# A fused attention and expert kernel: the SP queue and the scatters reordered, new weights for the order of steps, and the last two groups of heads taken by halves of the queries

## The reference, cut to what matters

```python
x = L0_attn_x
x = _layernorm(x + _L0_attn_ref(x, ...))      # 8 heads of 16, causal softmax, a rank-one term per head in the scores
x = _layernorm(x + _L0_ffn_ref(x, ...))

def _L0_ffn_ref(x, ...):
    x = x + mla_attention(rmsnorm(x, norm1_w), ...)   # latent of 64, 16 heads of 8, rotary, causal softmax
    x = x + moe(rmsnorm(x, norm2_w), ...)
    return x

def moe(x, gate_w, gate_b, W1, b1, W2, b2):
    logits = x @ gate_w.T + gate_b
    top = jnp.argmax(logits, axis=-1)
    onehot = jax.nn.one_hot(top, N_EXPERTS, dtype=x.dtype)     # 4 experts, hidden width 512
    h = jax.nn.relu(jnp.einsum('btd,ehd->bteh', x, W1) + b1)
    y = jnp.einsum('bteh,edh->bted', h, W2) + b2
    return jnp.einsum('btd,bte->btd', y, onehot)
```

## Time and profile before

| | |
|---|---|
| three runs, us | 559.97, 563.38, 565.47 (median 563.38) |
| the profiled execution | 565.1 us, its span in the trace 563.4 us |
| busy in the span | PE 480.2 us (85%), DVE 371.9 (66%), ACT 323.6 (57%), POOL 179.8 (32%) |
| granted PE clock, mean | 0.95 of full speed |

### The profile page before, as it was taken

One profiled execution on the slowest core, in us unless ns is written; L12 is line 12 of the kernel. 1 busy time (PEld: TensorE's weight loads), 2 busy tenths in 40 slices (PEclk: granted clock), 3 DMA queues, 4 the chain that ended last, 5 costly groups with the idle time before them and its releaser, 6 DMA issues.

```text
span 563.4 us, 10237 instructions
## 1 busy us (share of the span) xinstructions
PE 480.2 (85%) x3749; PEld 223.4 (40%) x3764; DVE 371.9 (66%) x690; ACT 323.6 (57%) x488; POOL 179.8 (32%) x249
## 2 busy tenths in 40 slices
PE   5576799998899989888797998848888988999993
PEld 3242233444442333333232333312554443367762
DVE  4286977788877889688888788866356721233343
ACT  3422156576676668867685776715456677843331
POOL 9830131237554237634030222452202304601000
PEclk9977889999999999999999799976899999999998
DMA  3894030306112002012010102031000000100010
GB/s 96 214 210 132 2 96 23 94 1 243 45 56 65 25 5 83 28 52 65 17 43 9 52 3 58 6 98 45 6 12 15 8 12 20 30 1 0 20 38 20
DMA packets 31571, 28.83 MB, mean 51 GB/s; under 512 B 8017, under 2 KB 27857, under 8 KB 31250
## 3 DMA queue, kind: packets, MB, share of 16 engines
q1 hardware_dynamic: 30626, 26.34, 16.3%
q0 software_dynamic: 896, 1.84, 1.4%
HBM read 19.27 MB, written 9.31 MB: 51 GB/s over the span
## 4 chain that ended last, share of the span: by engine, by line
PE 58%; ACT 10%; DVE 10%; SPq 8%; issue 5%; DMA 4%; POOL 3%; ACTq 1%; another core or an unknown queue 0%; DVEq 0%; POOLq 0%
PE ps L1407 15%; PE ps L1390 10%; ACT pr L1607 7%; PE ps L1370 7%; DVE mparts L1887 6%; PE ps L1486 5%; PE ps L1542 5%; SPq L1018 4%; PE ps L1472 3%; SPq L1088 3%; DMA qs<-nparts 2%; PE ps L1466 2%; PE ps L1586 2%; PE ps L1574 2%; PE ps L1418 2%
## 5 line engine op out<-in xcount | busy, mean ns | idle before, releaser
L1887 DVE TENSOR_REDUCE mparts<-ps 128x2 f32<-128x1024 f32 (+3 forms) x240 | 260.4, 1114 | 83.0 <-PE ps L1370 78.5
L1607 ACT ACTIVATE pr<-ps 128x1024 f32<-128x1024 f32 (+1 forms) x240 | 221.2, 939 | 142.9 <-PE ps L1390 140.6
L1407 PE MATMUL ps<-pr,vs 128*32 128x512 f32 (+3 forms) x1152 | 124.4, 506 | 9.1 <-ACT pr L1607 5.7
L1390 PE MATMUL ps<-qs,ks 64*128 64x512 bf16 (+7 forms) x561 | 102.1, 339 | 21.1 <-DMA qs<-nparts 11.3
L1370 PE MATMUL ps<-ks,qs 61*128 61x512 bf16 (+7 forms) x576 | 108.7, 348 | 4.0 <-DVE mparts L1887 1.9
L1208 POOL TENSOR_SCALAR_AFFINE_SELECT pr<-pr 128x512 f32<-128x512 f32 x96 | 60.7, 635 | 156.5 <-ACT pr L1607 156.3
L1390 PEld LDWEIGHTS ps<-qs,ks 64*128 64x128 bf16 (+1 forms) x576 | 31.5, 96 | 106.7 <-issue 41.6
L1370 PEld LDWEIGHTS ps<-ks,qs 61*128 61x128 bf16 (+1 forms) x576 | 35.5, 101 | 33.3 <-ACT pr L1607 11.0
L1407 PEld LDWEIGHTS ps<-pr,vs 128*32 128x32 f32 x1152 | 23.6, 108 | 48.5 <-issue 30.1
L1711 ACT ACTIVATE work<-ps,b 128x512 f32<-128x512 f32 x32 | 21.8, 685 | 29.7 <-PE ps L1542 28.2
L1363 PE MATMUL ps<-cmask,identb 64*128 64x128 bf16 (+1 forms) x96 | 23.4, 244 | 11.8 <-DVE mparts L1887 4.8
(11 more groups left out here) (174 smaller groups left out, 563.5 us busy)
## 6 DMA issues: line engine op xcount, KB each, us to landing
qs<-scr0q SPq DMA_DIRECT2D x48, 64.0 KB, 2.4
qs<-scr1q SPq DMA_DIRECT2D x84, 32.0 KB
ks<-scr1k SPq DMA_DIRECT2D x84, 32.0 KB
ks<-scr0k SPq DMA_DIRECT2D x36, 64.0 KB, 2.3
scr0q<-parts SPq DMA_DIRECT2D x4, 384.0 KB, 3.1
scr0k<-parts SPq DMA_DIRECT2D x4, 384.0 KB, 3.6
scr1q<-parts SPq DMA_DIRECT2D x4, 384.0 KB, 2.5
scr1k<-parts SPq DMA_DIRECT2D x4, 384.0 KB, 2.7
```

The costliest lines, as they stand in the source:

```text
L1390: last = pe.matmul(to[:, k, h, :], keys(F, 3, 2 * k + h0 + h, j * P, P), queries(F, 3, 2 * k + h0 + h, qb * 512 + lo, n), start=True, stop ...
L1407: last = pe.matmul(ps[VW * h:VW * (h + 1), PVB, lo:lo + n], vs[:, F % VSLOTS, j, VW * h:VW * (h + 1)], pr[:, st % PSLOTS, h, 0:n], start=( ...
L1607: act.activation(heads, scores_at(F, v), ACT.Exp, scale=GROUPS[F][0].scale).then_inc(exped, 1)
L1887: dve.tensor_reduce(heads, maxes_at(F, u), AX_X, ALU.max).then_inc(taken, 1)
```

## The change

The table of numbers that makes the list is new, and with it the places of most steps; beside that the diff changes these things.

- `query_halves()` and `SEQUENCE`: groups 10 and 11 are a pair (`PAIRED`). Their order is 10 q = 0, 11 q = 0, 10 q = 1, 11 q = 1. The maxima of group 11 are combined, turned and written in two halves, each with 12 DMAs (`rows`, four quarters of the rows). `serial()` gives the buffers of the exponentials in the new sequence; `ot` and `rc` alternate by it.
- `rows` of groups 4 to 10: three DMAs of two rows each in the place of six of one row.
- `MOST` allows three pairs of banks for scores and maxima and four single ones for the rest.
- The first half of group 0's keys is loaded from the SP queue, no longer from POOL.
- From the third on, a scatter waits until the one two before it has landed (two semaphores).
- `tile_out` on PE and `tile_relu` on ACT read the expert's number ahead of their waits.
- `hidden` waits for its own features, and is placed behind the last `tile_store`.

```diff
+PAIRED = [(10, 11)]
+ROWS_HALVED = [0] + [second for _, second in PAIRED]
...
-MOST = {"scores": 2, "row maxima": 2, "turns": 2, "side": 3}
+MOST = {"scores": 3, "row maxima": 3, "turns": 2, "side": 4}
...
+def query_halves():
+
+    out, F = [], 0
+    while F < NF:
+        groups = (F, F + 1) if (F, F + 1) in PAIRED else (F,)
+        out += [(G, q) for q in range(2) for G in groups]
+        F += len(groups)
+    return out
+
+
+SEQUENCE = query_halves()
+
+
+def serial(F, st):
+
+
+    k = SEQUENCE.index((F, STEPS[st][0]))
+    own = [s for s in range(NS) if STEPS[s][0] == STEPS[st][0]]
+    return sum(sum(STEPS[s][0] == q for s in range(NS)) for _, q in SEQUENCE[:k]) + own.index(st)
+
+
+SERIAL = {(F, st): serial(F, st) for F in range(NF) for st in range(NS)}
+STEP_OF_SERIAL = {n: step for step, n in SERIAL.items()}
+assert all(n % PSLOTS == st % PSLOTS for (F, st), n in SERIAL.items())
...
-    for F in range(NF):
-        passed, done = 0, {}
+    passed = 0
+    for F, q in SEQUENCE:
+        done = {}
         for v, (st, _, nh) in enumerate(UNITS):
-            out.append((F + passed / total, ("scores", F, v)))
-            passed += 2 * nh * STEPS[st][3]
-            done[st] = F + passed / total
-        for st in range(NS):
+            if STEPS[st][0] == q:
+                out.append((passed / total, ("scores", F, v)))
+                passed += 2 * nh * STEPS[st][3]
+                done[st] = passed / total
+        for st in done:
...
-            if st in END:
-                q = END.index(st)
-                out += [(done[st], ("evac", F, q)), (done[st], ("turn", F, q))]
+        out += [(done[END[q]], ("evac", F, q)), (done[END[q]], ("turn", F, q))]
...
-MAX_AHEAD, MAX_LENGTH = 1.2, 0.9
+MAX_AHEAD, MAX_LENGTH, SOONER = 1.2, 0.9, 0.25
...
-        first = F - (MAX_AHEAD if F else 1.0)
+        first = F - (MAX_AHEAD if F else 1.0) - SOONER * (F in ROWS_HALVED[1:])
...
-        for q in ((0, 1) if F == 0 else (2,)):
-            pos = first + MAX_LENGTH * (NX0 / NX if (F, q) == (0, 0) else 1)
+        for q in ((0, 1) if F in ROWS_HALVED else (2,)):
+            pos = first + MAX_LENGTH * (NX0 / NX if q == 0 else 1)
             out += [(pos, (kind, F, q)) for kind in ("combine", "turnmax", "rows")]
...
-FIRST = [[(-2.0, -1.5), (-1.6, -1.1)], [(-0.5, 0.0), (-0.1, 0.4)]]
-BETWEEN = [[(1.2, 1.21), (2.0, 2.01)], [(3.4, 4.9), (4.1, 5.6)]]
-READY = [[(7.4, 7.9), (8.1, 8.4)], [(11.4, 11.6), (12.1, 12.2)]]
-BY_ROWS = [(8.45, 11.5)]
+FIRST = [[(-2.0, -1.5), (-1.6, -1.1)], [(-0.53, -0.03), (-0.16, 0.34)]]
+BETWEEN = [[(1.27, 1.77), (1.7, 2.2)], [(3.81, 4.81), (4.05, 5.05)]]
+READY = [[(7.52, 7.92), (7.76, 8.06)], [(10.5, 10.7), (12.1, 12.2)]]
+BY_ROWS = [(8.38, 11.17)]
 RESULTS = [[(13.5, 13.6), (13.6, 13.7)], [(14.0, 14.1), (14.1, 14.2)]]
-EXPERTS = [[(7.9, 9.7), (9.7, 11.4)], [(11.6, 13.0), (13.0, 14.0)]]
+EXPERTS = [[(7.9, 9.7), (9.7, 11.4)], [(11.3, 12.83), (13.0, 14.0)]]
...
-URGENT = 0.6
-FEED, BACKLOG = 0.2, 2.0
-SP_IDLE = 5.0
+URGENT = 0.76
+FEED, BACKLOG = 0.32, 3.5
+SP_IDLE = 3.6
...
-         "combine": (DVE, 0.3), "rows": (SP, 1.0), "mask": (POOL, 0.64), "evac": (ACTE, 0.6), "y": (PE, 1.14),
...
+         "combine": (DVE, 0.3), "rows": (SP, 2.4), "mask": (POOL, 0.64), "evac": (ACTE, 0.59), "y": (PE, 1.14),
...
+def queue_of_load(F, k, half):
+
+    if F == 0 and k == 1:
+        return POOL if half == POOL_HALF else SP
+    return ACTE if F in ON_ACT else SP
...
-        queue = POOL if step[1:3] == (0, 1) else SP
-        return [(queue, 0.55 * len(PRODUCTS) if queue == POOL else 0.34 * len(PRODUCTS) * (1 + GROUPS[step[1]][0].n))]
+        queue = queue_of_load(*step[1:])
+        return [(queue, 0.55 * len(PRODUCTS) if queue == POOL else (0.47, 0.68)[GROUPS[step[1]][0].n] * len(PRODUCTS))]
...
+POOL_HALF = 1
+ON_ACT = ()
...
-            out.append(("scores", F - SLOTS, NU - 1))
+            out += [("scores", F - SLOTS, NU - 1), ("rows", F - SLOTS + 1, 2)]
...
-        if F == 0:
-            return [("rows", 0, int(UNITS[v][0] > END[0]))]
+        if F in ROWS_HALVED:
+            return [("rows", F, int(UNITS[v][0] > END[0]))]
...
-            before = (F, 0) if st > END[0] else (F - 1, 1)
-            out += [("evac", *before)] * (before[0] >= 0)
+            k = SEQUENCE.index((F, STEPS[st][0]))
+            out += [("evac", *SEQUENCE[k - 1])] * (k > 0)
...
-        return [("feat", "hat1", *a[:2]), ("lo", 15), ("v_proj", 1, 1, 1), ("moe_weights",)]
+        return [("feat", "hat1", *a[:2]), ("lo", 15), ("v_proj", 1, 1, 1), ("moe_weights",)] + [
+            ("tile_store", s, rows_of_tiles(s) - 1) for s in range(len(SORTED))]
...
-        scattered, collected_in = sem("scattered"), [sem(f"collected_in{i}") for i in range(2)]
+        scattered, collected_in = [sem(f"scattered{i}") for i in range(2)], [sem(f"collected_in{i}") for i in range(2)]
...
-                sp.wait_ge(scattered, 16 * len(tokens_of(s)))
+                for n in range(2):
+                    sp.wait_ge(scattered[n], 16 * len(tokens_of(s)) // 2)
...
+                        if q == 2:
+                            row = HALF - MAXIMA + p
+                            sp.dma_start(qs[row:row + HALF + 1:HALF, F % SLOTS, 0:2 * T], nparts[0:n, place, p, :]).then_inc(rows_in, 16)
+                            continue
                         for pair_of in range(2):
                             row = HALF * (pair_of + 1) - MAXIMA + p
-                            sp.dma_start(qs[row:row + 1, F % SLOTS, 0:2 * T],
-                                         nparts[2 * TB * pair_of:2 * TB * (pair_of + 1), place, p, :]).then_inc(rows_in, 16)
+                            for h in range(2):
+                                first = h * T + q * T // 2
+                                sp.dma_start(qs[row:row + 1, F % SLOTS, first:first + T // 2],
+                                             nparts[TB * pair_of + 4 * h:TB * pair_of + 4 * h + 4, place, p, :]).then_inc(
+                                    rows_in if q else rows_first, 16)
                         continue
...
+                if t >= 2:
+                    pool.wait_ge(scattered[t % 2], 16 * (t // 2))
...
-                                        xn[:, tokens_of(s)[t], :], None).then_inc(scattered, 16)
+                                        xn[:, tokens_of(s)[t], :], None).then_inc(scattered[t % 2], 16)
...
-                if F == 0 and UNITS[v] == (END[0] + 1, 0, 1):
-                    pe.wait_ge(rows_in, 48)
-                if v == 0:
-                    if F:
+                if F in ROWS_HALVED:
+                    if UNITS[v] == (END[0] + 1, 0, 1):
                         pe.wait_ge(rows_in, rows_value(F))
-                    else:
-                        pe.wait_ge(rows_first, 48)
+                    elif v == 0:
+                        pe.wait_ge(rows_first, 48 + 192 * ROWS_HALVED.index(F))
+                elif v == 0:
+                    pe.wait_ge(rows_in, rows_value(F))
...
-                if j == 4 * qb and (F or qb):
-                    pe.wait_ge(done["evac"], nth("evac", F, qb) - 1)
+                if j == 4 * qb and (F, qb) != SEQUENCE[0]:
+                    pe.wait_ge(done["evac"], SEQUENCE.index((F, qb)))
...
+                    if c == 0:
+                        pe.wait_ge(done["feat"], nth("feat", "hat1", b, i))
...
+                    e = pe.value_load(expert_of[0:1, j:j + 1], min_val=0, max_val=E - 1)
                     pe.wait_ge(done["tile_relu"], nth("tile_relu", s, j))
                     wait_bank(*step)
-                    e = pe.value_load(expert_of[0:1, j:j + 1], min_val=0, max_val=E - 1)
...
-                    if h0 == 0 and F * NS + st >= PSLOTS:
-                        act.wait_ge(done["pv"], F * NS + st - PSLOTS + 1)
+                    if h0 == 0 and SERIAL[F, st] >= PSLOTS:
+                        act.wait_ge(done["pv"], SERIAL[F, st] - PSLOTS + 1)
...
-                    act.copy(ot[:, q, :], ps[:, PVB, :]).then_inc(done["evac"], 1)
+                    act.copy(ot[:, SEQUENCE.index((F, q)) % 2, :], ps[:, PVB, :]).then_inc(done["evac"], 1)
...
+                    if j == 0:
+                        act.wait_ge(done["places"], nth("places", s))
+                    e = act.value_load(expert_of[0:1, j:j + 1], min_val=0, max_val=E - 1)
                     act.wait_ge(done["tile_hidden"], nth("tile_hidden", s, j))
...
-                    e = act.value_load(expert_of[0:1, j:j + 1], min_val=0, max_val=E - 1)
```

54 lines of the change are left out of this document (29 added, 25 removed).

## The result

The changed kernel takes 526.08 us (median of 4 runs, 523.18 to 526.83), the kernel before beside it 563.05 us. The ratio is 0.9337, with a 95% interval from 0.9277 to 0.9396: faster by 6.6%. In what follows, the gain of a version is (1 - its ratio) x 563 us, which takes out that the kernel before read 561.3 to 565.2 us in different comparisons; its interval is 1.5 to 3.4 us to each side, so a difference of two gains is uncertain by some 4 to 5 us.

The account below looks back on a forecast made before the run. PE bounds the kernel, busy 480.2 of 563.4 us. Terms 5 + 7 + 6 + 3.5 + 1.5 = 23 us, cut to three quarters, 17; 565.1 - 17 = 548, against the median 546 us, range 534 to 562.

Parts of the forecast that it names:

- The rest ... no sign, plus or minus 4: `MOST`, the new table and projections elsewhere reshuffle the body: no sign, plus or minus 4 us.
- They will not add in full ... I take three quarters: Over the whole sum of 23 us: DVE is next and pauses are partly found again, so 17 us.
- Start: Start of the kernel: earlier keys, rows and maxima of group 0 gain 5 us, range +2 to -10.
- Rows, groups 4 to 8: Group changes: three DMAs for six gain 1.3 us a group; with the order 7 us, range 0 to -11.
- Scatters: At the scatters: 6 us gained, range +3 to -12; sign PE busy over 12 of 16 us at clock 1.00.
- Registers: Tiles' output matmuls: reads ahead of the waits gain 3.5 us of 6.8 us idle, range 0 to -6.5.
- The pair: Groups 10 and 11: other matmuls fill PE's pauses between scores, 1.5 us gained, range +4 to -4.
- The dense end: End: attention's last scores later by some 10 us less the gain, the dense end shorter by it.
- the pauses go in full: Whole kernel: clock stays 1.00 from 52 us on, the whole 23 us and a few more, 537 us; chance 0.12.
- Found again: Body: a pause removed at the rows returns as a wait for a maximum, 557 us; chance 0.19.
- merged rows land late: Rows of maxima: two engines take 1.8 us longer than 16, the rows' term is 0, 551 us.
- the scatters' gate: POOL: masks of group 9 wait behind eight scatters, 567 us if a landing takes 10 us; chance 0.07.

Follow-up runs that it names:

- the fourth kernel: The changed kernel with the old numbers of the order and no pair, so only the code's edits are left: 547.43 us, ratio 0.9742.
- the first two experiments: The kernel before with one edit each: rows of maxima by three DMAs instead of six, 554.31 us; registers read ahead of the waits, 555.94 us.
- the third: The kernel before with one edit, each scatter from the third on waiting for the landing of the one two before: 562.58 us, ratio 1.0002.

## Why the prediction was wrong, by its own steps

The direction was right, and every stretch that a term stands for got shorter. The size failed at one step, and a second step came out right by luck.

**The step that failed is "The rest ... no sign, plus or minus 4".** I took the table of numbers for a reshuffle and gave it nothing. The numbers together are worth 37.3 - 17.3 = 20.0 us with the pair and 28.3 - 14.5 = 13.8 without it. That is also the size of the miss: the forecast's gain was 17 us, the measured one 37. The gains of groups 1 to 3 (5.6 us, of which the single edit of the rows gave 0.6) had no term at all. Which of the numbers gives the 20.0 us can't be said, because the halves of the table work only together (5.2, -6.8, together 20.0).

The profile before showed room for this. Its line for DVE's reductions (busy, mean ns; idle before them and its releaser) and PE's waits for them:

```profile
L1887 DVE TENSOR_REDUCE mparts<-ps 128x2 f32<-128x1024 f32 (+3 forms) x240 | 260.4, 1114 | 83.0 <-PE ps L1370 78.5
```

```profile
PE ps L1363 <- DVE mparts L1887: 4.8, 5, 2.7
...
PE ps L1390 <- DVE mparts L1887: 2.9, 9, 0.5
...
PE ps L1356 <- DVE mparts L1887: 2.5, 5, 1.1
...
PE ps L1370 <- DVE mparts L1887: 1.9, 4, 0.7
```

The reductions had 83.0 us of idle time ahead of them, 78.5 of it waiting for PE's maxima, while PE was idle 83.2 us itself. Only 12.1 us of PE's idle time were waits for these reductions, so the two did not simply wait for each other; but both had idle time that another order can fill, and the change edits the weight that prices DVE's backlog. DVE's 83.0 us became 39.6 in the changed kernel. I read the diff of the tables for where steps go and not for what the rule now weighs.

**The second step is "They will not add in full ... I take three quarters".** Its reason was that DVE is next. DVE did come near (90% in the body), and PE's waits for it before the scores rose from 2.9 to 7.7 us, in pieces of 0.3 us, but it didn't give back what the terms won: three single edits gave 14.2 us and together 14.5. Overlap was there between two other things, three DMAs and the new order, either of which hides the rows (7.9 us in the old order, 1.3 in the new). A flat factor over the sum was the wrong form for it. Its result, 17 us for the priced edits, agrees with the 17.3 measured, and that is luck: with the old numbers the start gave none of its 5 us (95.3 and 98.2 us, 95.5 before), and the registers gave 6.4 in place of 3.5. Without the cut the forecast would have been about 540, still 14 us too slow.

**Start** (5, seen 6.9): right in size, in mechanism half. SP's queue moved the way I walked it, if less far, but early first rows and early first scores alone give nothing. With the four weights old the first scores come earliest of all, and the start still takes 97.9 us:

```profile
40.51 0.81 PE L1441 MATMUL ps<-qs,ks 128*128 128x512 bf16 x3 [1.59 <-DMA qs<-nparts]
```

What goes with the short start is the second rows. In all twelve kernels with a start of 86.8 to 88.8 us they are issued between 55.9 and 60.6 us (59.35 in the changed kernel), in the eight others, at 94.8 to 98.2 us, between 67.4 and 71.1 (67.49 before). That these carry the gain is not isolated: the order of PE's maxima, on which they depend, moved with them.

**Rows, groups 4 to 8** (7): right in the old order. I had counted 1.3 us a group, 6.7 for the five changes, and the single edit gave 0.6 + 6.1 us there. The 9.4 us seen in the changed kernel are mostly not this term: with six DMAs in the new order groups 4 to 8 take 149.5 us in place of 148.6. My 0.5 us for a later landing was for nothing, and three DMAs take 1.59 us of SP and not 1.84. In the fourth kernel one wait for the merged rows is left and shows their landing:

```profile
368.03 1.59 SPq L1130 DMA_DIRECT2D qs<-nparts  x3
370.95 1.06 PE L1441 MATMUL ps<-qs,ks 64*128 64x512 bf16 x4 [1.06 <-DMA qs<-nparts]
```

The scores start 370.95 - 369.62 = 1.33 us after SP's last issue ends, and with one-row DMAs 250.70 - 249.37 = 1.33 us. In the old order the gaps behind one-row DMAs are 1.32 or 1.33 us at all five changes. By the section of the Trainium skill that the prediction cites (DMA: Bandwidth & Descriptors, on why a DMA increments its semaphore by 16) the merged rows go over two engines. No run here shows how many they use; in this kernel they land no later.

**Scatters** (6, seen 8.8 in the stretch): some 3 to 4 us of the 8.8 are the registers', so what is left is near the term. The sign that I gave didn't come. PE is busy over 12 of 16 us from 351 to 367, but the clock is 0.68 there and not 1.00: the stop at SP's queue is gone and another one, at DVE, stands in its place. The gating by itself is worth nothing.

**Registers** (3.5, seen 6.4 and 5.7): the mechanism was right and the size was half. I took half of the 6.8 us for a wait that the reads don't cause; 0.9 us were left.

**The pair** (1.5, seen 2.8 in the old order, 9.0 in the new): the pauses in the window of the earlier trace rows are gone as I said (PE busy 31.99 of 32 us, where it was 28.06). In the new order without the pair masks stand behind six gathers, and this I had not priced.

**The dense end** came as forecast: attention's last copy is 27.0 us earlier (492.7 to 465.7) and the whole 38.3, so that the end is 11.3 us shorter. Of the rivals, "the pauses go in full" (537) was nearest, with a chance of 0.12. "Found again" and "merged rows land late" are refuted in the old order by the first two experiments, the scatters' gate by the third.

What stays open: which of the numbers work together, and why weights, SP's costs and engines' costs lose more when old one by one than together (43 us against 26.8). The order is the outcome of a rule that picks one step after another, and I can't say which pick decides.

## What to carry to other kernels

When a change gives a scheduler new numbers, the order is a term of its own with a wide range, and not a rest without a sign: here it was 20.0 us beside 17.3 for all edits of code. How idle the engines next to the busiest one are shows what room there is (a suggestion that these runs do not test). Putting one number back to its old value tells what a mismatch costs and not what that number gave; to share out a gain, both halves have to be tried from the old side too. Add single terms in full, and take off an overlap only where two of them remove the same wait. And on an in-order queue look for rows of DMA starts ahead of a short step that the busiest engine needs: six gathers, 1.25 us apart, ahead of one mask cost about 8 us.

## What the runs showed of the hardware

The half clock behind a stop cost about as much as the stop: after 3.97 us without work PE ran at 0.56 and 0.80 over the next 16 us, by estimate up to 4.4 us more. After three DMAs of two rows each the waiting scores start 1.33 us behind the end of SP's last issue, the same as after six DMAs of one row. Register reads behind semaphore waits cost 6.4 us over 22 reads on two engines, 0.3 us a read, and 5.7 us in the other order of steps; with the reads ahead of the waits 0.9 of PE's 6.8 us of waiting were left. Two pairs of kernels with the same order of steps up to there differ in the start: the second half of group 0 is copied at 88.6 us in the changed kernel and at 86.8 with the old expert places, and at 98.2 and 95.3 us in the two kernels with old numbers. So single profiles can't tell 2 to 3 us there from nothing.
